# Node sums in a graph layer: one-hots as the stationary operand, messages in two halves, and a reordered opening

## The reference, cut to what matters

```python
xn = layernorm(x)                                       # 3125 x 256
msg = relu(xn[src] + edge_attr @ W_edge + b_edge)       # 50000 x 256
agg = segment_sum(msg, dst, 3125)                       # node sums
h = (1 + eps) * xn + agg
h = relu(batchnorm(relu(h @ W1 + b1) @ W2 + b2))
x = x + h + linear_attention(xn)
x = x + top2_of_8_experts(layernorm(x))
```

## Time and profile before

| | |
|---|---|
| median of 3 timed runs | 1014.28 us |
| profiled execution, its own time | 1009.37 us |
| its span (first to last instruction) | 1007.6 us |
| TensorE busy | 926.4 us (92%) |
| VectorE busy | 601.8 us (60%) |
| ScalarE busy | 538.3 us (53%) |
| GpSimd busy | 544.6 us (54%) |
| granted TensorE clock, mean | 0.967 of 2.4 GHz |

### The profile page before, as it was taken

The page is one execution under the profiler, slowest core; times in us unless marked ns, Lnnn a source line. Parts: engine busy times, 40 slices in busy tenths (PEclk is TensorE's granted clock), DMA queues, the critical chain, the costliest instruction groups (busy, mean ns, idle before and its releaser), DMA issues.

```text
span 1007.6 us, 17432 instructions
## 1 busy us (share of the span) xinstructions
PE 926.4 (92%) x6055; PEld 824.6 (82%) x6055; DVE 601.8 (60%) x1098; ACT 538.3 (53%) x1064; POOL 544.6 (54%) x527
## 2 busy tenths in 40 slices
PE   5899999999999999999999975379999999999995
PEld 4677889889888888897888765368999999999994
DVE  5555665565665565568989778835554454555442
ACT  2744545445545455445545564836555666555552
POOL 3277777777777777777774004023444444444433
PEclk8899999999999999999999998589999999999998
DMA  9667888877878878799775105459799789888722
GB/s 247 198 165 231 264 259 266 254 253 251 277 243 260 274 252 262 249 304 324 248 241 184 43 1 182 168 201 384 236 312 308 239 289 301 279 253 301 244 42 28
DMA packets 93173, 234.59 MB, mean 233 GB/s; under 512 B 20425, under 2 KB 37843, under 8 KB 84122
## 3 DMA queue, kind: packets, MB, share of 16 engines
q1 hardware_dynamic: 56694, 116.95, 33.9%
q0 software_dynamic: 29136, 64.72, 26.5%
q10 hardware_dynamic: 7252, 51.75, 12.8%
HBM read 183.81 MB, written 50.23 MB: 232 GB/s over the span
## 4 chain that ended last, share of the span: by engine, by line
PE 59%; POOL 13%; DMA 10%; DVE 8%; issue 7%; ACT 2%; DVEq 0%; POOLq 0%; SPq 0%; ACTq 0%
PE banks L1154 15%; POOL work L775 13%; PE banks L1174 10%; DMA work<-node_table,srcT 8%; PE banks L476 7%; PE banks L450 7%; PE banks L1176 5%; PE banks L924 3%; PE banks L983 2%; PE banks L439 2%; PE banks L1063 2%; PE banks L1051 1%; DVE work L526 1%; PE banks L1138 1%; DMA wts<-in_src 1%
## 5 line engine op out<-in xcount | busy, mean ns | idle before, releaser
L775 POOL DMA_INDIRECT work<-node_table,srcT x391 | 382.9, 979 | 151.6 <-issue 109.8
L498 ACT ACTIVATE work<-work 128x512 f32<-128x512 f32 x195 | 120.9, 630 | 127.0 <-DVE work L526 126.3
L476 PEld LDWEIGHTS banks<-work 128*128 128x128 f32 x1560 | 184.2, 192 | 4.5 <-DVE hT L544 1.1
L476 PE MATMUL banks<-work 128*128 128x128 f32 x1560 | 184.8, 275 | 0.7 <-DVE hT L544 0.7
L450 PE MATMUL banks<-w_edge,eaT 128*128 128x256 f32 x780 | 179.1, 379 | 0.0
L526 DVE TENSOR_TENSOR work<-banks,work 128x512 f32<-128x512 f32 x195 | 128.0, 682 | 69.5 <-DMA work<-node_table,srcT 55.1
L824 POOL DMA_INDIRECT out<-work,row_i x54 | 86.5, 1601 | 141.5 <-ACT work L1444 118.9
L1154 PE MATMUL banks<-xe_hi,wup 128*128 128x256 f32 x864 | 158.8, 285 | 3.8 <-DVE xe_lo L1901 3.8
L450 PEld LDWEIGHTS banks<-w_edge,eaT 128*128 128x128 f32 x780 | 143.1, 190 | 17.0 <-issue 0.2
L1174 PE MATMUL banks<-wdown,hid_hi 128*128 x432 | 155.9, 403 | 0.0
L1909 DVE TENSOR_TENSOR hid_lo<-wts,hid_hi 128x512 fp32r<-128x512 f32 x108 | 72.4, 691 | 134.7 <-ACT hid_hi L1421 134.7
(11 more groups left out here) (258 smaller groups left out, 1199.1 us busy)
## 6 DMA issues: line engine op xcount, KB each, us to landing
wup<-split_table ACTq DMA_DIRECT2D x24, 2048.0 KB, 9.7
work<-in_edge_attr SPq DMA_DIRECT2D x65, 384.0 KB, 5.1
wts<-in_L_ffn_W SPq DMA_DIRECT2D x64, 256.0 KB, 4.6
split_table<-raw_hi SPq DMA_DIRECT2D x64, 256.0 KB, 2.6
split_table<-raw_lo SPq DMA_DIRECT2D x64, 256.0 KB, 4.2
wdown<-split_table SPq DMA_DIRECT2D x8, 2048.0 KB, 9.7
work<-node_table,srcT POOLq DMA_INDIRECT x391, 4.5
wup<-split_table SPq DMA_DIRECT2D x3, 2048.0 KB, 8.2
```

The source lines that it names most:

```text
L476: last = nc.tensor.matmul(bank[5][:, h * P:(h + 1) * P], msg[:, u, j, h * P:(h + 1) * P], onehot[:, u, j], start=(j == 0), stop=(j == GT - 1))
L498: nc.scalar.activation(msg[:, u, 2 * q:2 * q + 2], msg[:, u, 2 * q:2 * q + 2], ACT.Relu).then_inc(msg_ready, 1)
L775: pool.indirect_dma_start(out=xg[i % RING][0:rows, j % 2], out_offset=None, in_=node_table, in_offset=bass.IndirectOffsetOnAxis(ap=srcT[0: ...
```

## The change

In the edge loop: the one-hot becomes the stationary operand and the messages the moving one, as two `fp32r` halves that sum to the message exactly. ScalarE's relu writes the high half into the space of `xs`; VectorE writes the low half in one new instruction for each group. The sums then come out with nodes on partitions, so ScalarE copies them out of PSUM and TensorE transposes them back. `aggregate` moves behind the attention matmuls of its iteration, `add_window` behind the second of three adds. The reload of `x` moves behind `edges_done`. In the opening: three list operations and two of the five bias adds go to GpSimd, and the statistics of all chunks come ahead of the lists' copies. The four semaphores of token buffers become two, with the same counts waited for in total.

```diff
-        onehot = view(work, 7680, 2, GT, P)
+        msg_lo = ...("msg_lo", [P, 2, GT, DIM], F32R, offset=work_offset + 4 * 4608)
+        msg_hi = ...("msg_hi", [P, 2, GT, DIM], F32R, offset=xs_offset)
+        sums = xs[:, 12]
+        onehot = ...("onehot", [P, 2, GT, P], F32R, offset=work_offset + 4 * 7680)
...
+        def aggregate(pe, n, u, fresh=False, tiles=GT):
             if not fresh:
                 pe.wait_ge(agg_read, n)
             pe.wait_ge(onehot_ready, n + 1)
+            pe.wait_ge(msg_low, n + 1)
+            for j in range(tiles):
+                for m in (msg_hi, msg_lo):
+                    last = nc.tensor.matmul(bank[5][:, 0:DIM], onehot[:, u, j], m[:, u, j],
+                                            start=(j == 0 and m is msg_hi), stop=(j == tiles - 1 and m is msg_lo))
+            last.then_inc(agg_ready, 1)
+
+        def turn_sums(pe, n):
+            pe.wait_ge(sums_copied, n + 1)
             for h in range(HALVES):
-                for j in range(GT):
-                    ...
-                    last = nc.tensor.matmul(bank[5][:, h * P:(h + 1) * P], msg[:, u, j, h * P:(h + 1) * P], onehot[:, u, j], ...
+                last = nc.tensor.transpose(bank[5][:, DIM + h * P:DIM + (h + 1) * P], sums[:, h * P:(h + 1) * P], ident[:])
+            last.then_inc(turned, 1)
...
+        def copy_sums(act, n):
+            act.wait_ge(agg_ready, n + 1)
+            nc.scalar.copy(sums, bank[5][:, 0:DIM]).then_inc(sums_copied, 1)
...
-                nc.scalar.activation(msg[:, u, 2 * q:2 * q + 2], msg[:, u, 2 * q:2 * q + 2], ACT.Relu
+                nc.scalar.activation(msg_hi[:, u, 2 * q:2 * q + 2], msg[:, u, 2 * q:2 * q + 2], ACT.Relu
...
+        def low_messages(dve, n, u, tiles=GT):
+            dve.wait_ge(msg_high, PAIRS * (n + 1))
+            nc.vector.scalar_tensor_tensor(out=msg_lo[:, u, 0:tiles], in0=msg[:, u, 0:tiles], scalar=0.0,
+                                           in1=msg_hi[:, u, 0:tiles].bitcast(F32), op0=ALU.max, op1=ALU.subtract
+                                           ).then_inc(msg_low, 1)
...
@@ SyncE
-                c = n - 2 * TILES - 1
-                if 0 <= c < CHUNKS:
-                    (load chunk c of x into xs)
...
             sp.wait_ge(edges_done, 1)
+            for c in range(CHUNKS):
+                (load chunk c of x into xs)
@@ GpSimd, ahead of the gathers
+            pool.wait_ge(ids_in, 64)
+            nc.gpsimd.tensor_copy(dst_f, dst_i).then_inc(rel_ready, 1)
+            nc.gpsimd.tensor_copy(src_f, src_i).then_inc(rel_ready, 1)
+            pool.wait_ge(low_known, 1)
+            nc.gpsimd.tensor_scalar(rel, dst_f, gstat[:, 0:1], None, ALU.subtract).then_inc(rel_ready, 1)
+            pool.wait_ge(small_in, 32)
+            for c in range(POOLED):                      # POOLED = 2
+                pool.wait_ge(xn_ready, CHUNK_TILES * (c + 1))
+                (table_stage of chunk c = xs + b_edge).then_inc(rows_pooled, 1)
@@ TensorE, edge loop
+                if n >= 2:
+                    turn_sums(pe, n - 2)
                 if n == DEN0:
                     attn_weights()
-                if n >= 1:
-                    aggregate(pe, n - 1, (n - 1) % 2, n == 1)
...                                                      (mix_kv, mix_q, mix_context, attn_den)
+                if n >= 1:
+                    aggregate(pe, n - 1, (n - 1) % 2, n == 1)
@@ ScalarE
+            nc.scalar.preload_act_table(ACT.Sqrt)
             normalise_x(0, LEAD[0])
             copy_xT(0)
             normalise_x(1, LEAD[1])
+            normalise_x(2, LEAD[2])
             copy_xT(1)
-            normalise_x(2, LEAD[2])
             copy_xT(2)
...
             for n in range(GROUPS):
+                if n >= 2:
+                    copy_sums(act, n - 2)
@@ VectorE, opening
-            (dst_f, min, clamp, rel, src_f)
             norm_of_x(1, LEAD[1])
-            add_bias(0)
+            dve.wait_ge(rel_ready, 1)
+            (min, clamp).then_inc(low_known, 1)
+            norm_of_x(2, LEAD[2])
             (iota_f and the five copies of the transposed lists)
-            norm_of_x(2, LEAD[2])
-            add_bias(0 .. 4)
+            for c in range(POOLED, CHUNKS):
+                add_bias(c)
@@ VectorE, edge loop
                 if n >= 2:
-                    add_window(dve, n - 2, ...)
+                    dve.wait_ge(agg_ready, n - 1)
                 (one-hot of group n, mix_k, attn_inverse)
+                add_nodes(dve, n, n % 2, range(PAIRS - 1))
+                if n >= 2:
+                    add_window(dve, n - 2, ...)           # now waits for turned
+                add_nodes(dve, n, n % 2, (PAIRS - 1,))
-                add_nodes(dve, n, n % 2)
                 (mix_q, round_low)
+                low_messages(dve, n, n % 2, 1 if last else GT)
```

More of the change, by code:

```diff
@@ L78 @@
 STAGES = 4
+POOLED = 2
 LEAD = ((0,), (1, 2), (3, 4))
@@ L307, in build @@
         sums_done = sem("sums_done")
-        msg_ready = sem("msg_ready")
+        msg_high = sem("msg_high")
+        msg_low = sem("msg_low")
+        sums_copied = sem("sums_copied")
+        turned = sem("turned")
         onehot_ready = sem("onehot_ready")
@@ L384, in build @@
         w_ready = sem("w_ready")
-        tok_in = [sem(f"tok_in{i}") for i in range(TOKS)]
+        tok_in = [sem(f"tok_in{u}") for u in range(2)]
         tok_T = sem("tok_T")
@@ L519, in add_tail, with add_nodes @@
             nc.vector.tensor_tensor(msg[:, u, 0], bank[2][:, 0:DIM], xg[i % RING][:, 0], ALU.add).then_inc(sums_done, PAIRS)
-        def add_nodes(dve, n, u):
-            for q in range(PAIRS):
+        def add_nodes(dve, n, u, pairs=range(PAIRS)):
+            for q in pairs:
                 i = PAIRS * n + q
@@ L680, in _ @@
             sp.wait_ge(edges_done, 1)
+            for c in range(CHUNKS):
+                for d, s in node_rows(a["x"], xs[:, c * CHUNK_TILES:(c + 1) * CHUNK_TILES], c):
+                    sp.dma_start(s, d).then_inc(x_again, 16)
             def store_x1(c):
@@ L715, in _ @@
             sp.wait_ge(lists_ready, 1)
-            for i in range(TOKS):
-                sp.wait_ge(tok_in[i], 16)
+            for u in range(2):
+                sp.wait_ge(tok_in[u], 16 * SUBS)
             for j in range(1, WUPS):
@@ L1014, in _ @@
                     attn_den((n - DEN0) // 2)
+                if n >= 1:
+                    aggregate(pe, n - 1, (n - 1) % 2, n == 1)
                 if n >= DEN0 + 3 and (n - DEN0 - 3) % 2 == 0:
                     attn_out((n - DEN0 - 3) // 2)
-            aggregate_tail(pe, GROUPS - 1, (GROUPS - 1) % 2)
+            turn_sums(pe, GROUPS - 2)
+            aggregate(pe, GROUPS - 1, (GROUPS - 1) % 2, tiles=1)
+            turn_sums(pe, GROUPS - 1)
             again = pe.value_load(miss_i[0:1, 0:1], min_val=0, max_val=1)
@@ L1030, in _ @@
                         aggregate(pe, n, 0)
+                        turn_sums(pe, n)
             with pe.Else():
@@ L1130, in tokens_turned @@
             def tokens_turned(j):
-                for s in range(SUBS):
-                    i = SUBS * j + s
-                    pe.wait_ge(tok_in[i % TOKS], 16 * (i // TOKS + 1))
+                pe.wait_ge(tok_in[j % 2], 16 * SUBS * (j // 2 + 1))
                 if j >= 1:
@@ L1321, in _ @@
                     nc.scalar.copy(w2_hi[:], w2[:]).then_inc(w12_high, 1)
+            for n in range(GROUPS - 2, GROUPS):
+                copy_sums(act, n)
             again = act.value_load(miss_i[0:1, 0:1], min_val=0, max_val=1)
@@ L1549, in _ @@
             nc.vector.tensor_copy(relT[:, GROUPS - 1, 0:1], bank[4][:, tail]).then_inc(tables_ready, 1)
-            norm_of_x(2, LEAD[2])
-            for c in range(1, CHUNKS - 1):
+            for c in range(POOLED, CHUNKS):
                 add_bias(c)
-            add_bias(CHUNKS - 1)
+            dve.wait_ge(rel_ready, 3)
             dve.wait_ge(weights_in, WEIGHT_DMAS * 16)
@@ L1624, in _ @@
                 if n >= 2:
-                    add_window(dve, n - 2, starts[(n - 2) % GT], mixed_by(n + 1), n == 2)
+                    dve.wait_ge(agg_ready, n - 1)
                 if last:
@@ L1641, in _ @@
                     attn_inverse(c, 2 * late)
+                if not last:
+                    add_nodes(dve, n, n % 2, range(PAIRS - 1))
+                if n >= 2:
+                    add_window(dve, n - 2, starts[(n - 2) % GT], mixed_by(n + 1), n == 2)
                 if last:
```

60 lines of the change are left out of this document (32 added, 28 removed).

## The result

The changed kernel takes 1090.38 us (median of 4 runs, 1088.09 to 1093.38) against 1014.25 for the kernel before on the same chip: 1.0753 times, interval 1.0731 to 1.0776. The prediction said 1056, 1028 to 1080. The direction is right, and the gathers are held as forecast, but the size is 34 us short: the holds cost more, and behind the 49 groups a wait appears that the prediction doesn't have.

A forecast was written before the change was run, and what follows sets the result against it. GpSimd's gathers and TensorE were taken to bound n up to 50, TensorE alone beyond. Opening -5, holds +37 and last stretch +10.5 gave +42 on 1014.3, about 1056 us; 1028 to 1080 holds 0.8.

The forecast's parts named there:

- What bounds the kernel: Edge loop: GpSimd's gathers and TensorE both at their limit for n = 1 to 50, TensorE alone beyond.
- The size of the hold, +37: Groups up to n = 50: the two-input low-half instruction holds gathers 0.75 us a group; 49 groups, +37 us (+12 to +73).
- free phase: Gathers start at any point of the low-half instruction: mean hold 0.98 us a group, +48 us over the 49 groups.
- The last stretch, +10.5: n = 52 to 64: VectorE's work and GpSimd's holds give 9.0 us a group against 8.19, +10.5 us (+6.5 to +17).
- The end of the loop, 0 (-1 to +2): Loop's end: copy and turn add about 1 us twice, 1.2 us of matmuls go; 0 us net.
- The opening, -5: Before the loop: statistics first and work moved to GpSimd bring the gathers 5 us earlier (-2 to -7), first gather near 38.
- The new instruction: VectorE in the loop: one 128 x 1536 low-half instruction a group takes 1.75 us and fits for n up to 50.
- the copy of the sums: ScalarE in the loop: copying 256 columns costs nothing under cover, about 0.4 us a group without it.
- the reload of `x`: After `edges_done`: 12 us of transfer within 40 us, hidden; at most 12 us on the path if that cover failed.
- Held longer: Rival, loop: the low half starts just before a gather each time, 1.3 us a group; 1088 us, chance 0.09.
- The clock: Rival, loop: waiting TensorE is granted 1.2 GHz for a quarter of the loop, 77 us more; 1130 us, chance 0.04.

## Why the prediction was right and wrong

- **What bounds the kernel** held. GpSimd's gathers set the pace for n up to 50. A lighter TensorE gave nothing there: it was busy 351.5 us instead of 365.9, and 328.0 in the version with the sums in PSUM, the order of before and a granted clock of 1.00. The 46 us more of gathers came through whole. The Trainium skill (SBUF — State Buffer, "Who interferes with whom") says that a VectorE instruction with two SBUF inputs contends with a GpSimd instruction that reads SBUF, and that one with at most one SBUF input, outside the two-port modes, doesn't. Every run here agrees: 63 of 64 held, and 44 of 45, against none of 66, 62 and 90. Its inference on descriptor generation does not agree with the 2.17 us of the gather above.
- **The size of the hold, +37, was the first step that failed.** The 49 groups got 47.2 us, 0.96 a group instead of 0.75. I had a mean over a free phase (0.98, +48) and narrowed it in two ways. The first was one phase, 0.8 us into the instruction, read from one group of the kernel before. In these groups of the changed kernel 50 gathers start inside L513, anywhere from 0.07 to 1.28 us after its start, 0.67 in the mean, so the phase was nearly free. The second was that the split of expert weights ahead of it might catch the gather before and so shorten the hold. The split held 14 gathers of these groups, 4.8 us together, and 15 in the kernel before, so nothing new came of that. L513 holds 50 gathers here, for 47.8 us together, and that is the free-phase figure.
- **The last stretch, +10.5, failed by a coupling that I didn't follow.** I summed VectorE's work and had 9.0 us a group against 8.19; with the window's add moved forward it is 120.64 / 14 = 8.6 against 110.83 / 14 = 7.9, +9.8. Both ends were too high, and that the difference lies near my term is partly luck. The other 11.3 us come with the wait of `aggregate` for `agg_read`, and go with it. With the add moved behind two adds, and those behind the embedding, the two engines wait for each other. I said of this wait nothing at all; the chain embedding, two adds, window, sums, attention output, embedding had to be summed like an engine.
- **The end of the loop, 0 (-1 to +2), was +8.7**, of which 1.3 us or more is the low 15.73 of the one profile of before. 4.0 of it goes with the same edit. Of the rest I saw the copy and the turn, but took them as 1 us twice. For the last three groups the chain matmul, copy, turn, add runs with nothing beside it, and VectorE waits 2.5, 1.5 and 1.6 us for it. With the float32 form for those groups the part takes 17.5 us, as much as in the other kernels of that form.
- **The opening, -5, was +1.8.** Statistics first did not bring the table earlier: chunk 1 itself landed late (VectorE waited 3.46 us for it at 16.45), and the two adds given to GpSimd held VectorE 4.6 us. I knew the rule in one direction and costed GpSimd's adds at nothing. The changed kernel's first gather is at 43.24, and then the first adds come late and the 13th gather waits for them. The version with the adds on VectorE has its first gather at 42.22, 0.8 us earlier, and its 13th at 58.64, where it was. No gather waits in it; two of the twelve are held by two-input instructions (1.31 and 1.70 us instead of 0.95), where the kernel before has one such (1.30), and that takes the 0.8 us back.
- **The new instruction, the copy of the sums and the reload of `x`** were costed rightly: 1737 ns (1.75 us predicted), no cost of the copy in the 49 groups (369.72 us with it, in the version with the sums in PSUM and the order of before), and no change from the reload and the table load alone.
- **The rivals.** "Held longer" (1088) came out nearest by its number, but not by its reason: it has 1.3 us a group from a fixed bad phase, and there was 0.96 from a free one. "The clock" (1130) was partly there, 0.93 granted for n up to 50, since keys and values waited for VectorE. It cost next to nothing: GpSimd's idle time in the stretch grew by 0.8 us, and at a clock of 0.98 the stretch was still 418.5 with the holds and 375.4 without.
- **What stays open** is the 10.6 us of TensorE's order in the changed kernel, which no profile places. The same move gave 6.7 us on the version with the sums in PSUM, 5.2 of them in the last stretch of its profile.

## What to carry to other kernels

Before giving VectorE an instruction beside a GpSimd that works without pause, count its SBUF inputs, and if there are two, find one that can stay in PSUM; in this kernel that was worth 33 us. Moving work off an engine that shares the bound with another gives nothing until the other moves too, and a form that pays in one stretch may be kept out of the next, where another engine sets the pace. When an edit moves the reader of a shared buffer to a later place, sum the loop through both engines that the buffer couples, not only each engine's work.

## What the runs showed of the hardware beyond that

The hold works in both directions: 0.18 us became 4.79 for a VectorE instruction of 10 elements a partition that started inside a GpSimd add of 2 x 1280. The very start is an exception: in the changed kernel and in the one with the added two-input instruction one gather each starts 0.03 us into the long instruction. Neither is held, and the instruction itself then takes 1.82 us instead of 1.74 or 1.75. The earliest of the held ones starts 0.07 us into it.

The keys and values matmuls of after, behind a wait of 3.88 us, run at half the clock (granted 0.50 from 316.7 to 320.5 us), and so do the first sums behind them, 0.21 us apart instead of 0.12. The same four matmuls in the kernel before, without such a wait, come last:

```profile
316.70 3.77 PE L953 MATMUL banks<-wkvT,qT 128*125 128x512 f32 x4 [3.88 <-DVE qT L1623]
...
320.48 0.41 PE L476 MATMUL banks<-msg_lo,onehot 128*128 128x256 f32 x1
320.70 0.41 PE L476 MATMUL banks<-msg_hi,onehot 128*128 128x256 f32 x1
```

```profile
299.95 1.88 PE L924 MATMUL banks<-wkvT,qT 128*125 128x512 f32 x4
```
